# A new order of work for one unit of relative attention: evictions ahead of the exps, bias rows and band earlier, probability transfers on SyncE

## The reference

```python
x = x + attn_a(layernorm(x))      # relative attention: the part that changes
x = x + ffn(layernorm(x))         # expert choice, 16 experts, and a shared part
x = x + attn_b(layernorm(x))      # windowed attention
x = x + ffn(layernorm(x))
```

```python
attn = q @ k^T                                         # q scaled
attn = attn + take_along_axis(q @ rpe_k_table, idx)    # idx = clip(j - i, -31, 31) + 31
attn = attn + swapaxes(take_along_axis(k * scale @ rpe_q_table, idx))
attn = softmax(attn)
out  = attn @ v + segment_sum(attn by bucket) @ rpe_v_table
```

## Time and profile before

| | us |
|---|---|
| median of 3 runs | 4486.95 |
| fastest and slowest of them | 4482.99 and 4490.35 |
| profiled execution, all of it | 4464.51 |
| its span, first to last instruction | 4462.7 |
| TensorE busy in the span | 3704.4 (83%) |
| VectorE busy | 2467.6 (55%) |
| ScalarE busy | 1833.0 (41%) |
| GpSimd busy | 784.6 (18%) |

### The profile page before, as it was taken

The page is one execution under the profiler, slowest core; times in us unless marked ns, Lnnn a source line. Parts: engine busy times, 40 slices in busy tenths (PEclk is TensorE's granted clock), DMA queues, the critical chain, the costliest instruction groups (busy, mean ns, idle before and its releaser), DMA issues. The chain is left out here.

```text
span 4462.7 us, 91470 instructions
## 1 busy us (share of the span) xinstructions
PE 3704.4 (83%) x32904; PEld 2935.2 (66%) x32904; DVE 2467.6 (55%) x5021; ACT 1833.0 (41%) x3784; POOL 784.6 (18%) x714
## 2 busy tenths in 40 slices
PE   4788888888886694799994799999999786599998
PEld 3455555555554584688883577777777676588887
DVE  4455555555554468565554455555454566755554
ACT  1455555555553230344441344444444331144443
POOL 0112212221121000233321010100101000133332
PEclk9899999999998896899996999999999788699999
DMA  4445455544554420444433100000000231244442
GB/s 173 135 133 140 137 150 136 146 135 131 149 144 130 155 80 12 138 124 119 124 90 115 48 12 15 11 13 12 11 15 14 83 118 50 81 120 126 113 113 52
DMA packets 383892, 423.79 MB, mean 95 GB/s; under 512 B 172896, under 2 KB 323296, under 8 KB 370016
## 3 DMA queue, kind: packets, MB, share of 16 engines
q1 hardware_dynamic: 223840, 319.05, 22.1%
q10 hardware_dynamic: 135168, 67.13, 5.4%
q0 software_dynamic: 24576, 33.57, 4.5%
HBM read 269.37 MB, written 150.27 MB: 94 GB/s over the span
## 5 line engine op out<-in xcount | busy, mean ns | idle before, releaser
L2005 PEld LDWEIGHTS a_ps_p<-a_ident,a_prob 128*128 128x128 f32 x2048 | 238.8, 144 | 251.3 <-ACT a_probT L2120 111.8
L2005 PE MATMUL a_ps_p<-a_ident,a_prob 128*128 128x128 f32 x2048 | 306.2, 284 | 107.1 <-ACT a_probT L2120 85.8
L2144 ACT ACTIVATE a_prob<-a_ps_s,a_low 128x512 f32<-128x512 f32 x512 | 327.0, 696 | 161.4 <-DVE a_low L2359 106.1
L2219 POOL TENSOR_TENSOR a_below<-a_probT,a_upper 128x512 f32<-128x512 f32 x128 | 165.6, 1294 | 1003.2 <-DVE a_probT L2342 551.0
L2359 DVE TENSOR_REDUCE a_low<-a_ps_s 128x2 f32<-128x1024 f32 x256 | 313.5, 1225 | 8.8
L2358 DVE TENSOR_TENSOR a_ps_s<-a_ps_s,a_win 128x320 f32<-128x320 f32 (+1 forms) x256 | 135.1, 528 | 275.4 <-PE a_ps_s L2038 139.3
L1476 ACT ACTIVATE b_prob<-b_score,b_low 128x256 f32<-128x256 f32 (+1 forms) x512 | 240.7, 474 | 27.0 <-PE b_ps_p L1418 23.8
L2120 ACT COPY a_probT<-a_ps_p 128x512 f32<-128x512 f32 x384 | 228.9, 596 | 21.3 <-PE a_ps_p L2005 21.3
L1428 PEld LDWEIGHTS b_ps_o<-b_v,b_probT 128*128 128x128 f32 x1792 | 227.2, 191 | 9.9 <-issue 0.9
L1428 PE MATMUL b_ps_o<-b_v,b_probT 128*128 128x64 f32 x1792 | 228.2, 267 | 0.7 <-DVE b_o L1562 0.7
L1549 DVE CUSTOM_DVE_ANT_0 b_score<-b_ps_s,b_bias 128x256 f32<-128x256 f32 (+1 forms) x512 | 184.8, 389 | 59.5 <-PE b_ps_s L1409 40.0
(11 more groups left out here) (400 smaller groups left out, 10645.7 us busy)
## 6 DMA issues: line engine op xcount, KB each, us to landing
a_win<-band SPq DMA_DIRECT2D x128, 384.0 KB, 5.5
prob<-a_prob ACTq DMA_DIRECT2D x128, 384.0 KB, 3.5
xnT<-n_xnT SPq DMA_DIRECT2D x32, 512.0 KB, 3.0
shift<-a_gbias SPq DMA_DIRECT2D x64, 256.0 KB, 2.1
a_shifted<-shift SPq DMA_DIRECT2D x256, 64.0 KB, 2.7
a_bins<-prob ACTq DMA_DIRECT2D x128, 128.0 KB, 3.8
fe_gT<-in_WgT SPq DMA_DIRECT2D x16, 1024.0 KB
fe_uT<-in_WuT SPq DMA_DIRECT2D x16, 1024.0 KB
```

Of the source, the lines that this page charges most:

```text
L2005: last = nc.tensor.transpose(bank[:, c * P:(c + 1) * P], prob[:, t % 2, h, 32 + c * P:32 + (c + 1) * P], ident[:, :])
L2144: nc.scalar.activation(prob[:, t % 2, h, 32:32 + T], ps_s[pair][:, r, :], ACT.Exp, bias=low[:, h:h + 1]).then_inc(exped, 1)
L2219: nc.gpsimd.tensor_tensor(below[:, t % 2, :, :], probT[:, t % 2, :, t * P:(t + 1) * P], upper[:, :].unsqueeze(1).to_broadcast([P, HG, P]), ...
```

## The change

`LEAD` raises k from 2 to 3 units. Within the unit the sections move: s_pos and s_neg are both in slot 0; band 0 and 1 go from slot 2 to slot 1; bins_T 0 and 1 go from the end of slot 2 to the end of slot 1, with v behind them, bins and out from slot 3 to slot 2, q from slot 3 to 2, k from slot 0 to 3, g_low and g_up from slot 2 to 3. On ScalarE all evictions but the third probs_T of a slot stand ahead of the slot's exps, and it issues no transfers any more: `prob_home` and `bins_home` are issued by SyncE. `bias_out` and `bias_back` are split by half. GpSimd's program is the same.

```diff
-LEAD = {"q": 3, "v": 2, "k": 2, "g_pos": 2, "g_low": 2, "g_up": 2, "s_neg": 1, "s_pos": 1, "band": 1, "bins_T": -1, "bins": -1, "out": -1}
+LEAD = {"q": 3, "k": 3, "v": 2, "g_pos": 2, "g_low": 2, "g_up": 2, "s_pos": 1, "s_neg": 1, "band": 1, "bins_T": -1, "bins": -1, "out": -1}
...
 RELATIVE_ORDER = [
-    ("scores", 0), ("k", 0), ("probs_T", 0), ("probs_T", 1), ("values", 0), ("s_pos", 0), ("probs_T", 2), ("lower", 0), ("probs_T", 3),
...
+    ("scores", 0), ("probs_T", 0), ("probs_T", 1), ("values", 0), ("probs_T", 2), ("s_pos", 0), ("lower", 0), ("probs_T", 3), ("s_neg", 0),
+    ("scores", 1), ("band", 0), ("band", 1), ("probs_T", 4), ("probs_T", 5), ("g_pos", 0), ("values", 1), ("probs_T", 6), ("lower", 1), ("probs_T", 7),
+    ("bins_T", 0), ("bins_T", 1), ("v", 0),
+    ("scores", 2), ("probs_T", 8), ("probs_T", 9), ("values", 2), ("probs_T", 10), ("bins", 0), ("lower", 2), ("probs_T", 11), ("q", 0), ("out", 0),
+    ("scores", 3), ("probs_T", 12), ("probs_T", 13), ("g_low", 0), ("values", 3), ("probs_T", 14), ("g_up", 0), ("lower", 3), ("probs_T", 15), ("k", 0),
 ]
 RELATIVE_VECTOR_ORDER = [
...
+    ("max", 0), ("max", 1), ("s_pos", 0), ("probs_T", 3), ("s_neg", 0),
+    ("max", 2), ("max", 3), ("probs_T", 6), ("probs_T", 7), ("o", 0), ("v", 0), ("x", 0),
+    ("max", 4), ("max", 5), ("bins", 0), ("probs_T", 11), ("out", 0),
+    ("max", 6), ("max", 7), ("g_up", 0), ("probs_T", 15),
 ]
...
+                home(b, g, 0)
+                if has_step(b, g, "band", 0):
+                    bias_back(*unit_after(b, g, 1), 0)
+                home(b, g, 1)
                 if has_step(b, g, "band", 0):
                     band_rows(*unit_after(b, g, 1))
+                if has_step(b, g, "g_pos", 0):
+                    bias_out(*unit_after(b, g, 2), 1)
+                home(b, g, 2)
                 if has_step(b, g, "band", 0):
                     windows(*unit_after(b, g, 1))
+                if has_step(b, g, "g_pos", 0):
+                    bias_back(*unit_after(b, g, 2), 1)
...
+                home(b, g, 3)
                 if has_step(b, g, "out", 0):
                     store(*unit_before(b, g, 1))
+                if has_step(b, g, "g_up", 0):
+                    bias_out(*unit_after(b, g, 2), 0)
...
-                    pe.wait_ge(emptied, section(b, g, "s_pos") + 1)
+                    pe.wait_ge(emptied, section(b, g, "s_neg") + 1)
...
-                    elif kind == "home":
-                        home(*tile_before(b, g, k, 1))
```

More of the change, by code:

```diff
@@ L1592 @@
 RELATIVE_PROLOGUE = [
-    ("q", 0, 0), ("k", 0, 0), ("g_low", 0, 0), ("g_up", 0, 0), ("g_pos", 0, 0),
-    ("q", 1, 0), ("k", 1, 0), ("v", 0, 0), ("s_neg", 0, 0), ("s_pos", 0, 0), ("band", 0, 0), ("band", 0, 1),
-    ("g_low", 1, 0), ("g_up", 1, 0), ("g_pos", 1, 0), ("q", 2, 0),
+    ("q", 0, 0), ("k", 0, 0), ("g_pos", 0, 0), ("g_low", 0, 0), ("g_up", 0, 0), ("q", 1, 0), ("k", 1, 0), ("v", 0, 0),
+    ("s_pos", 0, 0), ("s_neg", 0, 0), ("band", 0, 0), ("band", 0, 1), ("g_pos", 1, 0), ("g_low", 1, 0), ("g_up", 1, 0),
@@ L1596 @@
+    ("q", 2, 0), ("k", 2, 0),
 ]
 RELATIVE_ORDER = [
-    ("scores", 0), ("k", 0), ("probs_T", 0), ("probs_T", 1), ("values", 0), ("s_pos", 0), ("probs_T", 2), ("lower", 0), ("probs_T", 3),
-    ("scores", 1), ("g_pos", 0), ("probs_T", 4), ("probs_T", 5), ("values", 1), ("s_neg", 0), ("probs_T", 6), ("lower", 1), ("probs_T", 7), ("v", 0),
-    ("scores", 2), ("g_low", 0), ("probs_T", 8), ("probs_T", 9), ("values", 2), ("g_up", 0), ("band", 0), ("band", 1), ("probs_T", 10), ("lower", 2), ("probs_T", 11),
@@ L1609 @@
-    ("g_low", 0), ("probs_T", 8), ("home", 2), ("exp", 4), ("probs_T", 9), ("band", 0), ("exp", 5), ("band", 1), ("probs_T", 10),
-    ("x", 0), ("bins_T", 0), ("bins_T", 1),
-    ("q", 0), ("probs_T", 12), ("home", 3), ("exp", 6), ("probs_T", 13), ("exp", 7), ("probs_T", 14),
+    ("probs_T", 0), ("probs_T", 1), ("exp", 0), ("exp", 1), ("probs_T", 2), ("x", 0),
+    ("band", 0), ("band", 1), ("probs_T", 4), ("probs_T", 5), ("g_pos", 0), ("exp", 2), ("exp", 3), ("bins_T", 0), ("bins_T", 1),
+    ("probs_T", 8), ("probs_T", 9), ("exp", 4), ("exp", 5), ("probs_T", 10),
@@ L1612 @@
+    ("q", 0), ("probs_T", 12), ("probs_T", 13), ("g_low", 0), ("exp", 6), ("exp", 7), ("probs_T", 14), ("k", 0),
 ]
 RELATIVE_VECTOR_ORDER = [
[L1614 to L1617, removed]
+    ("max", 0), ("max", 1), ("s_pos", 0), ("probs_T", 3), ("s_neg", 0),
+    ("max", 2), ("max", 3), ("probs_T", 6), ("probs_T", 7), ("o", 0), ("v", 0), ("x", 0),
@@ L1869, in load_x, with bias_out, bias_back @@
                 sp.dma_start(xT[:, :, :], by_channel(xnT_d, b)).then_inc(xT_in, 16)
-            def bias_out(b, g):
+            def bias_out(b, g, i):
                 u = NG * b + g
[L1874 to L1881, removed]
-                u = NG * b + g
[L1884 to L1892, removed]
+                if not (isinstance(u, int) and u == 0):
+                    hold(sp, shifted_in[i], 16 * HG * u, held)
+                hold(sp, emptied, section(b, g, "g_pos" if i else "g_up") + 1, held)
+                sp.dma_start(scratch["shift"][i][:, 32:32 + T], gbias[:, i, :]).then_inc(gbias_out[i], 16)
+            def bias_back(b, g, i):
+                u = NG * b + g
+                if not (isinstance(u, int) and u == 0):
+                    hold(sp, emptied, section(*unit_before(b, g, 1), "s_pos" if i else "s_neg") + 1, held)
+                hold(sp, gbias_out[i], 16 * u + 16, held)
+                for h in range(HG):
+                    rows_at = scratch["shift"][i]
+                    skewed = bass.AP(rows_at.tensor, rows_at.offset + 32 * h * R + 32 * i, [[R + 1, 32], [1, T]])
+                    sp.dma_start(shifted[32 * h:32 * h + 32, i, :], skewed).then_inc(shifted_in[i], 16)
             def band_rows(b, g):
@@ L1917, in store, with prob_home, bins_home, home @@
                 sp.dma_start(out, o[:, g % 2, :, :, :].rearrange("p t h d -> p t (h d)")).then_inc(o_out[g % 2], 16)
+            def prob_home(b, g, t):
+                n = tile_number(b, g, t)
+                hold(sp, exped, HG * n + HG, held)
+                if not (isinstance(n, int) and n < 2):
+                    hold(sp, bins_in[t % 2], 16 * (2 * (NG * b + g) + t // 2), held)
+                sp.dma_start(scratch["prob"][t % 2].rearrange("p (h x) -> p h x", h=HG),
+                             prob[:, t % 2, :, t * P:t * P + WIN]).then_inc(prob_out[t % 2], 16)
+            def bins_home(b, g, t):
+                hold(sp, prob_out[t % 2], 16 * (2 * (NG * b + g) + t // 2 + 1), held)
+                src = scratch["prob"][t % 2]
+                skewed = bass.AP(src.tensor, src.offset, [[W4 + 1, P], [WIN, HG], [1, XB]])
+                sp.dma_start(bins[:, g % 2, t, :, :], skewed).then_inc(bins_in[t % 2], 16)
+            def home(b, g, t):
+                n = NG * b + g
+                if not (isinstance(n, int) and n == 0 and t < 1):
+                    prob_home(*tile_before(b, g, t, 1))
+                if not (isinstance(n, int) and n == 0 and t < 2):
+                    bins_home(*tile_before(b, g, t, 2))
             load_x(0)
@@ L1927, in unit @@
             def unit(b, g):
[L1928 to L1933, removed]
+                home(b, g, 0)
+                if has_step(b, g, "band", 0):
+                    bias_back(*unit_after(b, g, 1), 0)
+                home(b, g, 1)
                 if has_step(b, g, "band", 0):
                     band_rows(*unit_after(b, g, 1))
-                if has_step(b, g, "k", 0):
-                    bias_back(*unit_after(b, g, 2))
+                if has_step(b, g, "g_pos", 0):
+                    bias_out(*unit_after(b, g, 2), 1)
+                home(b, g, 2)
                 if has_step(b, g, "band", 0):
                     windows(*unit_after(b, g, 1))
+                if has_step(b, g, "g_pos", 0):
+                    bias_back(*unit_after(b, g, 2), 1)
+                if g == 0 and not (isinstance(b, int) and b == B - 1):
+                    hold(sp, emptied, section(b, 2, "v") + 1, held)
+                    load_x(b + 1)
+                home(b, g, 3)
                 if has_step(b, g, "out", 0):
                     store(*unit_before(b, g, 1))
-            bias_out(0, 0)
-            bias_back(0, 0)
+                if has_step(b, g, "g_up", 0):
+                    bias_out(*unit_after(b, g, 2), 0)
+            bias_out(0, 0, 1)
+            bias_out(0, 0, 0)
+            bias_back(0, 0, 1)
+            bias_back(0, 0, 0)
             band_rows(0, 0)
-            bias_out(0, 1)
+            bias_out(0, 1, 1)
             windows(0, 0)
-            bias_back(0, 1)
+            bias_back(0, 1, 1)
+            bias_out(0, 1, 0)
             units(nc.sync, unit)
+            prob_home(B - 1, NG - 1, NT - 1)
+            bins_home(B - 1, NG - 1, NT - 2)
+            bins_home(B - 1, NG - 1, NT - 1)
             store(B - 1, NG - 1)
@@ L2144, in exp @@
```

(4 more changed lines are left out.)

7 lines of the change are left out of this document (removed).

## The result

The changed kernel takes 4582.81 us (median of 4 runs, 4577.59 to 4586.74); the kernel before took 4484.97 beside it. The ratio is 1.0222, with a 95% interval of 1.0196 to 1.0248: slower by 2.2%, where 4585 was forecast. The profiled execution has a span of 4584.6 us.

A forecast was written before the change was run, and what follows sets the result against it. Bound by TensorE's work, 31.8 us a unit, plus some 5 us of waits. 31.7 + 3.6 + 1.6 + 3.3 + 0.2 = 40.4, with v 41.4, with clock 42.9 against 39.64: +98 us over thirty units, 4585; range 4440 to 4680.

The forecast's parts named there:

- The lateness of the sums: GpSimd's band sums, behind slot 2's mask, end 9.8 and 11.4 us into slot 2; SyncE waits before band_rows.
- The stall of slot 3, +3.6: First exp of slot 3 waits for tile 1's probability transfer, queued on SyncE behind band_rows: 3.6 us a unit.
- The exps of slot 0, +1.6: Exps of slot 0 wait for tile 2's probabilities, sent behind the windows: 1.6 us a unit.
- the landing taken as 5.8: Probability transfer home(3), issued behind windows and s_pos bias rows, lands after 5.8 us, between 3.5 and 7.9.
- s_neg, +3.3: SyncE waits for tile 1's bins, so s_neg's bias rows and TensorE's band transposes come 3.3 us a unit later.
- The clock, +1.5: Three TensorE idle stretches a unit lower its clock, costing 1.5 us a unit, bounds 0 and 4.
- The gain without stalls, 32.7 us a unit: With nothing else late, the new slots take 32.7 us a unit instead of 37.1: 4.4 us less.
- rival E: Nothing queued on SyncE matters: 34.2 us a unit with 1.5 for the clock, -163 us, 4324; chance 0.04.
- B: Transfers land at their unloaded medians, so exps of slot 0 lose nothing: +17 us, 4504; chance 0.22.
- C: Only slot 3's stall remains; exps of slot 0 and s_neg rows are on time: -55 us, 4432; chance 0.15.
- D: Clock and landing both bad: 45.4 us a unit, +173 us, 4660; chance 0.12.

The follow-up runs named there:

- kernel 1: The changed kernel with GpSimd's two band sums right behind the mask of slot 1 instead of slot 2: 4303.92 us, ratio 0.9633.
- kernel 2: The changed kernel with GpSimd's band sums ahead of the mask of slot 1, instead of behind the mask of slot 2: 4253.50 us, ratio 0.9522.
- kernel 3: The changed kernel with the probability transfers back on ScalarE, GpSimd's order as in the changed kernel: 4542.59 us, ratio 1.0163.
- kernel 7: kernel 2 with the probability transfers on ScalarE: 4314.12 us, ratio 0.9662.
- Kernel 6: The changed kernel with bias_back of s_neg ahead of home(0) on SyncE: 4534.50 us, ratio 1.0158.
- kernel 4: The changed kernel with home(2) and bias_out of g_pos ahead of band_rows on SyncE: 4545.70 us, ratio 1.0187.
- kernel 5: The kernel before, with GpSimd's band sums ahead of the mask of slot 2 instead of behind it: 4378.91 us, ratio 0.9800.

## Why the prediction was right

Its steps against the unit shown above, in us after the scores of slot 2 (754.95). The prediction left v out of this replay and added it at the end, and the unit shown makes no v in its slot 1:

| step | predicted | measured |
|---|---|---|
| mask starts | 7.1 | 6.9 |
| first band row issued | 9.9 | 9.7 |
| strip of tile 1 issued | 13.7 | 14.3 |
| exps of slot 3 | 17.3 | 17.4 |
| scores of slot 0 | 19.9 | 20.0 |
| strip of tile 2 issued | 20.0 | 20.5 |
| exps of slot 0 | 25.8 | 25.7 |
| scores of slot 1 | 28.4 | 28.3 |
| home(0), behind tile 1's bins | 26.5 | 27.6 |
| s_neg | 32.1 | 32.7 |
| band transposes | 33.0 | 33.6 |
| scores of slot 2 | 40.4 | 42.2 |

**The lateness of the sums**: right, and shown as the cause by kernels 1 and 2. It came from reading GpSimd's program, which the diff doesn't touch, against TensorE's new order.

**The stall of slot 3, +3.6**: right. The scores of slot 0 come 12.2 us after those of slot 3, as forecast 11.85.

**The exps of slot 0, +1.6, and the landing taken as 5.8**: right; the strip issued at 775.42 landed after 5.2 us, the bins issued at 776.06 after 6.4. In the 18 units from 300 to 1100 us the strip of home(3), the one behind the windows, landed after 4.1 to 7.7 us, median 5.2, and every other strip after 3.0 to 4.7. The five that took 7.0 us and more stand in the units where a load of x (512 KB) is issued just ahead of it, which the prediction didn't mention. The rule of the Trainium skill (DMA: Bandwidth & Descriptors, Queues, rings and completion order) that the DMA engines take turns between queues was given no price, and no run here measures it: kernels 3 and 7 change the queue and the order of issue together.

**s_neg, +3.3**: right in place and size (the band transposes waited 3.91), incomplete in its cause. The prediction named tile 1's bins. Kernel 6 takes that wait away and the landing of the g_up rows takes its place 2 us sooner; both are ends of the same burst. In the unit shown they already lie side by side: the bins landed at 782.5, and the g_up write, issued at 777.62, landed after 5.9 us, at 783.5, just before SyncE came to the bias rows at 784.04. The prediction gave that write no time.

**The clock, +1.5**: direction right. The last step of the table is 1.2 us longer than the replay from the band transposes on, and the clock in that stretch was 0.66:

```profile
790.00:794.00 4.00, 4.00 (x42) 2.79 (x42) 1.78 (x3) 2.19 (x5) 0.00 (x0) 0.66 0.02 4
```

It is the mean of 4 us that start 1.5 us after TensorE's 3.91 us of idle. No run measures the clock's cost by itself, so 1.5 stays an estimate that fits. An estimate of its upper bound: TensorE is busy 35.0 us a unit here (650.58 of 800, times 43.06) and 31.7 in kernel 2 for the same work at 1.00, so the lower clock stretched that work by some 3.3 us a unit, part of it where the engine would have waited anyway. For the kernel before, the same sum gives 33.4 - 31.7 = 1.7 us, where the prediction put down the whole 2.6 us between 39.64 and 37.07 to the clock. That reading is not shown; it enters neither the 42.9 nor the forecast.

**The gain without stalls, 32.7 us a unit**: 32.4 in kernel 2, with nothing left for the clock: its mean is 1.00 from 300 to 1100 us. The prediction had added 1.5 for it in its rival E, and so placed that case at 4324; 0.9522 of 4484.97 is 4271, some 50 us below that. In kernel 2 TensorE idles at most 1.4 us at a time for another engine and the mean granted clock stays at 1.00, so in that case the term should have been nothing.

**What was read wrongly** is how the terms combine. The prediction added three stalls as if each had a price of its own. Kernels 3, 4 and 6 each take one or two away and get back 1.2, 1.2 and 1.3 us a unit between profiled runs, and 0.5 to 1.2 by the medians and ratios, under half of the price. They are one round that begins at the late sums and comes back to slot 2, along several strands of nearly the same length. The sum was right because the whole chain had been followed; a part of it was not to be had by a part of the fix. That also fits with kernels 3, 4 and 6 coming out slower than expected, and kernel 1 faster.

**How near, and how much of it is luck.** The mechanism was right, but the 2 us between 4585 and 4582.81 are partly luck. The medians differ by 97.8 us where 98 was forecast; the stage itself grew by 110.6 us between the two profiled runs, and 11 us more came from stages whose code is the same. The profiled run of the kernel before was also faster than all four runs that the ratio rests on (4464.51 against 4471.83 at the least). The changed kernel's unit, 42.7 and 43.1 in its two profiled runs against 42.9, is the better measure of the forecast. Two slips in the prediction change nothing: 5.08 + 1.3 + 0.14 makes 6.5 us at least for a slot, not 6.6, and a third of B's 0.22 is 0.07, not 0.09.

**Rivals.** B (landings at their medians) was refuted by 5.2 and 6.4 us. C needed SyncE at the s_neg rows by 23.1 us after the scores of slot 2; it came at 29.1 (784.04). D came nowhere near. E did not happen in this kernel, but describes kernel 2.

## What to carry to other kernels

When steps move between slots, look up every engine whose program the diff leaves alone and ask at which step it reads the moved work: here four GpSimd instructions, still in their old place, turned a gain of 4.8% into a loss of 2.2%. A transfer moved to an in-order queue takes on the wait of everything ahead of it, so ask first when the queue's longest wait ends. And when stalls form one round, remove its head: here removing one link gave back 0.5 to 1.3 us a unit, and removing the head 9.1 to 10.7.

## What the runs showed of the hardware

A transfer issued right behind others of a burst landed later than the same transfer elsewhere: 4.4 us against a median of 2.1 for the 256 KB write, 5.2 against 3.5 for a strip (7.0 us and more with a 512 KB load issued just ahead as well), 6.4 against 3.8 for the bins. The changed kernel's strips as a whole were not slower than before (median 3.3 us against 3.5). The TensorE clock stood at 1.00 on average from 300 to 1100 us with TensorE 98% busy, at 0.99 with 87% (kernel 5), and at 0.90 with 81%, where it had two idle stretches in each unit, of 3.5 to 4.7 and of 0.4 to 5.5 us. The busy share alone doesn't tell it: with 84% in both, the kernel before had 0.96 and kernel 4 had 0.87.
